# The second residual of a fused Mamba and RWKV layer: a VectorE add in place of TensorE's identity matmuls and ScalarE's copy

## The reference

```python
x = x + L0_attn(layernorm(x))     # projections, 16-state scan, gate, W_out, layernorm
x = x + L0_ffn(layernorm(x))      # the second residual

# in L0_attn, per token:  h = dA_t * h + dBx_t ;  y_t = sum over 16 states of h * C_t
# in L0_ffn:
r = sigmoid(xr @ W_r)
k_act = square(relu(xk @ W_k))
out = r * (k_act @ W_v)
```

## Time and profile before

| what | value |
|---|---|
| time, median of 3 runs | 942.09 us (941.38 to 942.38) |
| the profiled execution, its own time | 944.42 us |
| its span, first to last instruction | 942.6 us |
| VectorE (DVE) busy | 900.9 us, 96% of the span |
| GpSimd (POOL) busy | 889.1 us, 94% |
| TensorE (PE) matmuls busy | 864.2 us, 92% |
| ScalarE (ACT) busy | 847.9 us, 90% |
| mean granted TensorE clock | 0.973 |

### The profile page before, as it was taken

How to read it: one execution, slowest core, us unless ns; L and a number is a source line. 1 busy time by engine, 2 the same in 40 slices (tenths; PEclk the granted TensorE clock), 3 DMA queues, 4 the chain that set the end, 5 groups by cost and what they waited for, 6 DMA issues and landing times.

```text
span 942.6 us, 15838 instructions
## 1 busy us (share of the span) xinstructions
PE 864.2 (92%) x5024; PEld 688.7 (73%) x5024; DVE 900.9 (96%) x985; ACT 847.9 (90%) x2064; POOL 889.1 (94%) x399
## 2 busy tenths in 40 slices
PE   8757679999999899989999899998999999999998
PEld 5545567877878587787868678786778768778876
DVE  4899989999999999999999999999999999999896
ACT  5886988989999999998999999999999999978875
POOL 4999999999999999999999989999999999999970
PEclk9987898999999999999999999999999999999999
DMA  7445435462534644455463644446354354446231
GB/s 222 156 177 204 175 138 204 179 235 104 210 157 161 239 164 172 183 178 166 174 248 147 224 148 160 179 179 248 125 210 179 143 198 179 157 160 223 91 101 45
DMA packets 49938, 163.60 MB, mean 174 GB/s; under 512 B 5248, under 2 KB 33152, under 8 KB 33600
## 3 DMA queue, kind: packets, MB, share of 16 engines
q1 hardware_dynamic: 48528, 161.27, 46.2%
q0 software_dynamic: 512, 1.31, 0.5%
q10 hardware_dynamic: 816, 0.02, 0.1%
HBM read 153.15 MB, written 9.44 MB: 172 GB/s over the span
## 4 chain that ended last, share of the span: by engine, by line
PE 46%; ACT 28%; DVE 15%; issue 9%; DMA 1%; POOL 0%; POOLq 0%; DVEq 0%; SPq 0%; ACTq 0%
PE w_ps L1326 10%; ACT da_ps L654 10%; PE y_ps L1317 9%; PE w_ps L1350 6%; DVE da_ps L1033 5%; PE w_ps L1359 4%; PE w_ps L1362 4%; DVE hg L1049 3%; DVE hg L1033 3%; PE w_ps L1465 3%; DVE hg L1040 2%; PE w_ps L1368 2%; ACT xn_tok L591 2%; ACT h_tok L591 2%; ACT zs L715 2%
## 5 line engine op out<-in xcount | busy, mean ns | idle before, releaser
L542 POOL TENSOR_TENSOR dbx<-u,b_ring 128x1024 f32<-128x1024 f32 x255 | 599.4, 2380 | 4.7 <-DVE hg L1033 4.6
L654 ACT ACTIVATE da_ps<-delta,a_neg 128x512 f32<-128x512 f32 x512 | 340.0, 684 | 23.9 <-DVE hg L1040 7.3
L555 POOL TENSOR_TENSOR hg<-hg,c_ring 128x1024 f32<-128x1024 f32 x122 | 290.4, 2381 | 8.5 <-ACT carry L660 6.7
L1317 PE MATMUL y_ps<-ident,hg 128*128 128x128 f32 x2048 | 264.3, 279 | 9.2 <-POOL hg L555 9.0
L1317 PEld LDWEIGHTS y_ps<-ident,hg 128*128 128x128 f32 x2048 | 241.7, 145 | 35.9 <-issue 17.8
L1033 DVE TENSOR_TENSOR_SCAN da_ps<-da_ps,carry,dbx 128x512 f32<-128x512 f32 x203 | 249.8, 1271 | 4.3 <-ACT da_ps L654 4.1
L1033 DVE TENSOR_TENSOR_SCAN hg<-da_ps,carry,dbx 128x512 f32<-128x512 f32 x181 | 220.3, 1263 | 1.4 <-ACT carry L660 1.2
L1040 DVE TENSOR_TENSOR hg<-da_ps,c_ring 128x1024 f32<-128x1024 f32 x68 | 82.3, 1210 | 0.2
L1049 DVE TENSOR_TENSOR hg<-da_ps,c_ring 128x512 f32<-128x512 f32 x130 | 82.3, 673 | 0.0
L1033 DVE TENSOR_TENSOR_SCAN da_ps<-da_ps,dbx 128x512 f32<-128x512 f32 x64 | 75.8, 1213 | 3.3 <-ACT da_ps L654 2.8
L1326 PE MATMUL w_ps<-xnT_ring,w_in 128*128 128x512 f32 x120 | 61.4, 636 | 16.0 <-ACT xT L696 14.1
(11 more groups left out here) (212 smaller groups left out, 1333.0 us busy)
## 6 DMA issues: line engine op xcount, KB each, us to landing
c_ring<-bc_rows_dram SPq DMA_DIRECT2D x64, 1024.0 KB, 4.7
b_ring<-bc_rows_dram SPq DMA_DIRECT2D x63, 1024.0 KB, 6.7
xres<-in_L_attn_x_in_dram SPq DMA_DIRECT2D x16, 512.0 KB, 4.8
x_tok<-in_L_attn_x_in_dram SPq DMA_DIRECT2D x15, 512.0 KB, 5.9
out_dram<-r_out SPq DMA_DIRECT2D x14, 512.0 KB, 3.2
bc_rows_dram<-bc_rows SPq DMA_DIRECT2D x64, 16.0 KB, 5.4
w_in<-in_L_attn_W_in_dram SPq DMA_DIRECT2D x2, 256.0 KB, 4.3
x_tok<-in_L_attn_x_in_dram SPq DMA_DIRECT2D x2, 256.0 KB, 4.6
```

The source lines that it names most:

```text
L542: pool.tensor_tensor(dbx[:, n % X_RING, :, :], u[:, ip, :, :], b.to_broadcast([P, KH, LC]), ALU.mult).then_inc(s["dbx_done"], 1)
L555: pool.tensor_tensor(part, part, c_of(n).to_broadcast([P, KH, LC]), ALU.mult).then_inc(s["g_pool"], 1)
L654: act.activation(da_of(n, h), delta[:, ip, h, :], ACT.Exp, scale=a_neg[:, h, n:n + 1]).then_inc(s["da_ready"], 1)
L1317: last = pe.matmul(y_tok[:, b, h * P:(h + 1) * P], hg[:, n % H_RING, h, b * P:(b + 1) * P], ident[:, :], is_transpose=True, start=n == 0 a ...
```

## The change

The second residual is added by VectorE. A new `add_residual(v, c)` reads the gated value from the PSUM bank and `xres` from SBUF and writes `r_out`; it frees the bank. It stands at VectorE's place 31, behind both `out_of` (in the last step at place 19). TensorE's `xo0` and `xo1`, ScalarE's `ev0` and `ev1`, and the semaphores `out_ready` between them go. Nothing else moves.

```diff
-                sum30=25, sum31=27, sum3_set=28, sq3=28, rs3=29, ev0=31, ev1=31, norm3=31)
-VEC_TURN = dict(mix1=5, mix0=6, gate=8, z0=12, z1=16, u0=17, u1=22, x20=24, x21=25, v0=31, v1=31)
+                sum30=25, sum31=27, sum3_set=28, sq3=28, rs3=29, norm3=31)
+VEC_TURN = dict(mix1=5, mix0=6, gate=8, z0=12, z1=16, u0=17, u1=22, x20=24, x21=25, v0=31, v1=31, add0=31, add1=31)
-               x1=6, wo1=7, wo0=7, k1=7, xa1=9, xa0=9, xD=10, v0=12, v1=12, xo0=13, xo1=13)
+               x1=6, wo1=7, wo0=7, k1=7, xa1=9, xa0=9, xD=10, v0=12, v1=12)
...
-VEC_TAIL = dict(mix1=2, mix0=2, gate=6, x21=15, x20=15, v1=17, v0=18, late_mix1=20, late_mix0=20)
+VEC_TAIL = dict(mix1=2, mix0=2, gate=6, x21=15, x20=15, v1=17, v0=18, add0=19, add1=19, late_mix1=20, late_mix0=20)
...
-                    for v in range(2):
-                        if end and at(f"ev{v}"):
-                            need(act, out_ready[v], t - 1)
-                            act.activation(r_out[:, 2 * v:2 * v + 2, :], by_block(bank(t, f"v{v}")),
-                                           ACT.Copy).then_inc(read_sem(t, f"v{v}"), 1)
+                def add_residual(v, c):
+                    part = r_out[:, 2 * v:2 * v + 2, :]
+                    need(dve, s[f"gv{v}_done"], c + 1)
+                    need(dve, ln_sum[3], c + 1)
+                    dve.tensor_tensor(part, by_block(bank(t, f"v{v}")), xres[:, c % 2, 2 * v:2 * v + 2, :],
+                                      ALU.add).then_inc(read_sem(t, f"v{v}"), 1)
...
+                    for v in range(2):
+                        if end and at(f"add{v}"):
+                            add_residual(v, t - 2)
-                    for v in range(2):
-                        if end and n == turn[f"xo{v}"]:
-                            need(pe, s[f"gv{v}_done"], t - 1)
-                            need(pe, ln_sum[3], t - 1)
-                            for j in range(2):
-                                last = pe.matmul(by_block(bank(t, f"v{v}"))[:, j, :], ident[:, :], xres[:, t % 2, 2 * v + j, :],
-                                                 start=False, stop=True, skip_group_check=True)
-                            last.then_inc(out_ready[v], 1)
```

More of the change, by code:

```diff
@@ L58 @@
 ACT_TAIL = dict(prev=0, hT1=2, hT0=2, tanh=8, gT1=9, gT0=9, k1=11, sq20=12, sq21=13, rs2=14, k0=15, sum31=16,
-                late_prev=16, square=16, sum30=16, sum3_set=16, sq3=16, rs3=17, norm3=18, ev1=18, late_hT0=19,
-                late_hT1=19, ev0=22, late_k1=24, late_k0=27, late_square=27, late_tanh=31)
-VEC_TAIL = dict(mix1=2, mix0=2, gate=6, x21=15, x20=15, v1=17, v0=18, late_mix1=20, late_mix0=20)
-PE_TAIL = dict(hT0=0, hT1=0, r0=2, r1=2, gT0=3, gT1=3, wo0=4, wo1=4, k1=4, k0=5, xD=6, xa0=6, xa1=6, xo1=7, v0=7,
-               v1=7, late_hT1=9, xo0=9, late_hT0=9, late_k1=12, late_r0=12, late_k0=12, late_r1=13)
+                late_prev=16, square=16, sum30=16, sum3_set=16, sq3=16, rs3=17, norm3=18, late_hT0=19,
+                late_hT1=19, late_k1=24, late_k0=27, late_square=27, late_tanh=31)
+VEC_TAIL = dict(mix1=2, mix0=2, gate=6, x21=15, x20=15, v1=17, v0=18, add0=19, add1=19, late_mix1=20, late_mix0=20)
+PE_TAIL = dict(hT0=0, hT1=0, r0=2, r1=2, gT0=3, gT1=3, wo0=4, wo1=4, k1=4, k0=5, xD=6, xa0=6, xa1=6, v0=7,
+               v1=7, late_hT1=9, late_hT0=9, late_k1=12, late_r0=12, late_k0=12, late_r1=13)
 TAIL_BANK = dict(v1=2, v0=1, late_r1=1, hT0=0, k1=2, late_hT1=0, gT1=1, r0=1, hT1=1, r1=0, late_k0=0, k0=0,
@@ L216, in mamba_rwkv_layer @@
         ln2_g = [sem(f"ln2_g{v}") for v in range(2)]
-        out_ready = [sem(f"out_ready{v}") for v in range(2)]
         ln_nr = {ln: sem(f"ln{ln}_nr") for ln in nm}
```

## The result

The changed kernel takes 971.39 us (median of 4 runs, 969.38 to 974.03) where the one before takes 942.24: a ratio of 1.0308, with a 95% interval of 1.029 to 1.0325. It is slower, as forecast, but by 29 us and not by 14; 971.4 lies outside the range of 948.5 to 960.0. The profiled execution reads 974.03 us, with a span of 972.2.

A forecast was written before the change was run, and what follows sets the result against it. VectorE was taken to bound the steps. Adds of 16.5 us less 2.4 us given back made 14.1 us, so 942.09 became 956.2 us; forecast 953 to 959.5 (0.70), 8-in-10 range 948.5 to 960.0.

The forecast's parts named there:

- The bound: VectorE was said to bound the steps, idle 6.2 us in twelve whole steps, 0.5 us in a step of 55.5 us.
- The adds: On VectorE, 28 adds at 0.59 us from start to start, 16.5 us in all, without waits for its own results.
- TensorE's matmuls: Eight removed per step, 26.7 us busy, ahead of TensorE's wait for ScalarE's norm; claimed gain: nothing.
- ScalarE's copies: Two removed per step, 13 us in all; VectorE was to get back 0.8, 1.3 and 0.3 us.
- The 0.12 us at the boundary: VectorE's delay at a step boundary from ScalarE's copies holding back column 1's exponential; 0.8 us over twelve boundaries.
- the 1.32 us at the last boundary: VectorE's late scans at the boundary to the last step, behind a delayed exponential; the whole 1.32 us was to go.
- The last step: Its adds stand in a stretch where VectorE has no idle time, so they were to be paid in full.
- The sum: 16.5 us added on VectorE less 2.4 given back, 14.1 us, on a median of 942.09.
- 0.3 given back: Behind the last boundary, 0.3 us less of VectorE's wait for ScalarE's shift of h.
- The rivals: Four: more given back (0.15), adds at full duration (0.08), faster because ScalarE's copies set boundaries (0.03), no change (0.04).
- Rival A: Freed ScalarE and TensorE remove up to 10.8 us of VectorE's idle time: 947.8 us, likelier 949 to 953; chance 0.15.

## Why the prediction was wrong

**The bound.** Right where the clock holds: VectorE sets the steps, and what it does more, it pays for in full. In the kernel after, it also waits 1.5 us a step, which the prediction didn't expect.

**The adds.** Right: 0.59 us each from start to start, and no wait for the engine's own results.

**TensorE's matmuls: the step that failed.** The prediction said "Less work ahead of such a wait lengthens the wait. Gain: nothing, and the cover is that wait." The first sentence was right, and with it I took the matter for settled. A longer wait isn't free on this engine. Alone, the removal costs 8.3 us of the stretch. In the changed kernel it meets the adds, which lengthen the same wait from the other side, 2.0 us become 4.8 to 5.1, and the clock falls at twelve boundaries and not at four. Against the kernel with four matmuls put in, that is 16.6 us of the stretch, 1.4 at a boundary.

**ScalarE's copies.** Right in size, though not as a gain by itself. The 0.12 us at the boundary went, the 1.32 us at the last boundary went, and ScalarE's lead ended at the next exponential. Tried alone, the relief brings nothing. In the changed kernel the sum below comes out with it, but no run takes it out there.

**The last step.** The prediction had it paid in full and nothing more. In the kernel after VectorE waits 2.37 us there where it waited 0.53:

```profile
890.88 1.91 PE L1321 MATMUL y_ps<-ident,hg 128*128 128x128 f32 x8 [2.19 <-POOL hg L554]
...
900.60 0.60 ACT L722 ACTIVATE r_out<-w_ps 128x512 f32<-128x512 f32 x1 [1.76 <-PE w_ps L1366]
...
903.23 1.29 DVE L1026 TENSOR_TENSOR_SCAN da_ps<-da_ps,carry,dbx 128x512 f32<-128x512 f32 x1 [2.37 <-ACT da_ps L653]
```

```profile
890.00:892.00 2.00, 1.12 (x6) 1.12 (x7) 2.00 (x4) 1.89 (x4) 2.00 (x2) 0.75 0.12 28
892.00:894.00 2.00, 2.00 (x8) 1.72 (x7) 2.00 (x3) 0.81 (x2) 2.00 (x2) 0.50 0.94 360
```

TensorE, early by the removed matmuls, waits for GpSimd; the clock falls to 0.50; the matmuls of r end late; ScalarE's tanh waits for them; an exponential stands behind the tanh, and VectorE waits for it. In the kernel before the clock is 1.00 from 862 to 870 us, the same part of the step. Three other kernels that lack the identity matmuls show the same (VectorE waits 2.36 us in the changed kernel with four put in, 1.82 with the matmuls alone left out, 2.5 with these left out and four put in), and the kernels that have them show 0.5 to 0.7.

But two kernels lack the matmuls and don't show it: the changed kernel with two put in, and the one with the norm moved. In the first of them:

```profile
880.89 1.09 PE L1321 MATMUL y_ps<-ident,hg 128*128 128x128 f32 x8 [2.20 <-POOL hg L554]
...
891.56 1.29 DVE L1026 TENSOR_TENSOR_SCAN da_ps<-da_ps,carry,dbx 128x512 f32<-128x512 f32 x1 [0.70 <-ACT da_ps L653]
```

```profile
882.00:884.00 2.00, 2.00 (x11) 1.74 (x11) 2.00 (x3) 0.81 (x2) 2.00 (x2) 1.00 0.97 389
```

TensorE waits as long as in the kernel after, at the same place, but here the clock holds at 1.00, and VectorE's wait is 0.70 us. The program of the last step is the same in both. So the missing matmuls make TensorE's idle time, and by these rows it is the fall of the clock that makes VectorE's wait longer; behind 2.2 us the clock may fall or hold. No kernel had this gap filled, so this is a comparison of rows and not a run of its own.

**The sum.** With the clock held at the step boundaries of both, the change costs 716.3 - 701.7 = 14.6 us of the stretch. By the terms: 13 pairs at 1.18 are 15.3, less 0.8, 1.3 and 0.3 given back, and 1.65 more for the wait in the last step (2.36 for 0.71), together 14.6. The last term is the clock again; without it the forecast's own terms, which for the 13 pairs of this stretch give 12.9 of its 14.1, come out. By the medians the change costs 955.09 - 939.54 = 15.6, or 14.4 if each is taken against the kernel before as it was measured with it (943.88 and 942.70). What the forecast lacked is the clock at the boundaries: 16.6 us lost by the changed kernel, and 2.9 that the kernel before was losing already. 14.6 + 16.6 - 2.9 = 28.3, the growth of the stretch from 704.6 to 732.9. The adds were sized rightly, and by their mechanism, and the size of ScalarE's relief fits. The miss is the term of the removed matmuls, put at nothing: in this stretch it is 28.3 - 12.9 = 15.4 us, a part of which needs the adds too. The median missed its forecast by 971.4 - 956.2 = 15.2.

**The rivals.** None of the four was it. Each moved work between engines at fixed durations. That TensorE's matmuls take longer behind an idle time (1.94 us for 0.98) had no place in the sum. The cue was there: the dips to 0.50 stand in the trace of before, at the very wait that the change was going to lengthen, with a shift wait of VectorE behind each. Rival A even counted these waits as something that the change might give back.

## What to carry to other kernels

When a change takes work from TensorE just ahead of a wait, look at how long that wait is and what the granted clock does behind it now; the saving can turn into matmuls at 1.2 GHz on the path of the engine that binds. A few matmuls that nobody reads, put into a bank that is free at that point and sized a little under the idle time, are a cheap test of whether the clock is the cause. Two of them in the kernel before are also a gain of 0.3%. Moving the conditional work to another place in the order was no cure here, where another engine sets the period: the idle time turned up at the next condition. And a clock that holds behind a wait in one profile doesn't show that the wait is short enough: behind the same 2.2 us in the last step it fell in some kernels and held in others.

## What the runs showed of the hardware

Behind an idle time of 2.0 to 2.1 us the clock fell at four of twelve boundaries of the same kernel and held at eight; behind 4.8 to 5.1 us it fell at all twelve. Behind 2.2 us in the last step it fell in three kernels (after, after with four put in, before with the matmuls left out) and held in two (after with two put in, and with the norm moved). In the kernel after it was still at 0.50 in the stretch from 435 to 437 us, though TensorE had taken up work again at 431.16 and is shown as busy since. At that level the eight 128x128 transposes of the norm took 1.94 us, and at the higher one seven of them took 0.98. Removing 26.7 us of matmuls made TensorE's own busy time 2.6 us less.
